# Top-32 selection of two heads in turns, and another order of the work behind the last heads

## The reference, cut

```python
scores = einsum('bthd,bghd->bhtg', Q, K) / sqrt(DH)       # 4 heads of 32, 2048 context rows
topv, topi = top_k(scores, 32); probs = softmax(topv)
attn_mean = zeros_like(scores).at[..., topi].set(probs).mean(axis=1)
c_t = einsum('btg,bgd->btd', attn_mean, x_vision @ Wv)
x = layernorm(x_text)
scale_in, shift_in = split(c_t @ W_film_in + b_film_in)
x = x * (1 + mod_gate * scale_in) + mod_gate * shift_in
K = 2 * einsum('dn,dnl->dl', dC, exp(dtA * arange(L))).real
y = irfft(rfft(x) * rfft(K)) + x * D_skip
scale_out, shift_out = split(c_t @ W_film_out + b_film_out)
y = y * (1 + mod_gate * scale_out) + mod_gate * shift_out
```

## Time and profile before

| what | value |
|---|---|
| median of three runs | 783.0 us (781.75 to 784.87) |
| the profiled execution | 782.62 us, span 780.8 us |
| busy share PE, DVE, ACT, POOL | 87%, 48%, 35%, 29% |
| chain that ended last | PE 63%, DVE 16%, POOL 9%, ACT 6%, issue 3%, DMA 2% |
| mean granted TensorE clock | 0.906 |

### The profile page before, as it was taken

How to read it: one execution, slowest core, us unless ns; L and a number is a source line. 1 busy time by engine, 2 the same in 40 slices (tenths; PEclk the granted TensorE clock), 3 DMA queues, 4 the chain that set the end, 5 groups by cost and what they waited for, 6 DMA issues and landing times.

```text
span 780.8 us, 10116 instructions
## 1 busy us (share of the span) xinstructions
PE 681.5 (87%) x3848; PEld 320.2 (41%) x3848; DVE 374.8 (48%) x1179; ACT 273.1 (35%) x580; POOL 227.5 (29%) x146
## 2 busy tenths in 40 slices
PE   4948659878478799999999999989799999999997
PEld 2314235334244354444444444545554333333343
DVE  5988879998997335561002341534662111001114
ACT  1867868879778110013120001545111001111010
POOL 2479767856957920000000000000140000000012
PEclk9976677868568899999999999999799999999999
DMA  9971320702704851006005014001958999999923
GB/s 289 292 280 40 107 82 7 263 1 83 281 0 161 264 222 40 1 0 216 0 7 209 0 39 177 1 1 47 384 199 303 389 375 346 372 373 369 382 80 126
DMA packets 63521, 132.94 MB, mean 170 GB/s; under 512 B 8368, under 2 KB 18544, under 8 KB 62960
## 3 DMA queue, kind: packets, MB, share of 16 engines
q1 hardware_dynamic: 59072, 122.91, 43.6%
q0 software_dynamic: 1920, 6.29, 2.8%
q10 hardware_dynamic: 2480, 3.08, 1.2%
HBM read 121.86 MB, written 8.32 MB: 167 GB/s over the span
## 4 chain that ended last, share of the span: by engine, by line
PE 63%; DVE 16%; POOL 9%; ACT 6%; issue 3%; DMA 2%; ACTq 0%; DVEq 0%; POOLq 0%
PE PS L1675 8%; PE PS L1650 7%; PE PS L1471 7%; PE PS L1491 7%; PE PS L1389 6%; PE PS L1243 4%; DVE KA L949 4%; PE PS L1508 4%; PE PS L1670 4%; PE PS L1655 4%; DVE AR L990 2%; PE PS L1505 2%; POOL TT L434 2%; PE PS L1319 1%; DVE V L958 1%
## 5 line engine op out<-in xcount | busy, mean ns | idle before, releaser
L415 POOL TENSOR_TENSOR RS<-VE,CST 128x1 f32<-128x1 f32 (+1 forms) x18 | 11.2, 621 | 268.7 <-DVE VE L912 266.4
L1276 PE MATMUL PS<-AR,WK 128*128 128x512 f32 x96 | 54.7, 726 | 17.3 <-DMA AR<-in_ctxT 17.3
L949 DVE MAX8 KA<-AR 128x8 f32<-128x64 f32 x512 | 66.4, 210 | 2.4 <-issue 2.0
L1214 DVE COPY AR<-PS 128x512 f32<-128x512 f32 (+1 forms) x9 | 5.9, 668 | 124.3 <-PE PS L1243 124.3
L1675 PE MATMUL PS<-AR,TT 128*32 128x512 f32 x512 | 60.3, 593 | 1.5 <-issue 1.4
L567 POOL DMA_INDIRECT AR<-expert_rows,SLU x8 | 8.3, 1034 | 181.0 <-DMA expert_rows<-XT 178.9
L1650 PE MATMUL PS<-AR 128*32 128x512 f32 x512 | 57.9, 594 | 0.9 <-ACT AR L863 0.6
L1471 PE MATMUL PS<-TT,AR 128*128 128x512 f32 (+2 forms) x144 | 55.5, 546 | 3.3 <-ACT TT L791 3.3
L1293 PE MATMUL PS<-AR,QT 32*128 32x512 f32 x128 | 43.3, 759 | 16.8 <-ACT AR L600 15.9
L1389 PE MATMUL PS<-AR 128*128 128x512 f32 x128 | 56.1, 594 | 0.3 <-DVE XT L1115 0.3
L1491 PE MATMUL PS<-AR 128*128 128x512 f32 x128 | 55.5, 593 | 0.9 <-ACT AR L800 0.9
(11 more groups left out here) (290 smaller groups left out, 1205.7 us busy)
## 6 DMA issues: line engine op xcount, KB each, us to landing
AR<-in_w SPq DMA_DIRECT2D x32, 2048.0 KB, 12.4
AR<-in_ctxT SPq DMA_DIRECT2D x16, 768.0 KB, 8.1
AR<-in_ctx SPq DMA_DIRECT2D x16, 768.0 KB, 7.9
AR<-in_W SPq DMA_DIRECT2D x2, 4096.0 KB, 12.9
token_rows<-AR SPq DMA_DIRECT2D x1, 2560.0 KB, 11.0
X<-in_x SPq DMA_DIRECT2D x2, 1024.0 KB, 5.5
AR<-AR POOLq DMA_DIRECT2D x8, 256.0 KB, 3.4
AR<-in_W_film_in SPq DMA_DIRECT2D x4, 512.0 KB, 11.4
```

The source lines that it names most:

```text
L949: last = eng.max(CAND[0][:, n, :], s[:, n * G // NCH:(n + 1) * G // NCH])
L1276: last = mm(PS[:, 4 + n % 2, :], WK[:, j, :], CXT[slot][:, j, :], start=j == 0, stop=j == KV - 1)
```

## The change

It does five things.

1. The two heads of a pair are selected together. `thresholds(m, found)` alternates between them, with candidates in CAND[0] and CAND[1] and what is left in LEFT[0] and LEFT[1] (in KB); `Chain.put` signals, `Chain.after` waits later. VectorE's order in a pass is maxima of the first head, `whole` in late passes, a masked product of the pair before, maxima of the second head, the other masked product, `diagonal` in late passes, thresholds, settle.
2. `exponentials` makes both heads' scaled maxima and both logarithms with one instruction each; the two shifts follow each other without a wait.
3. At the end VectorE does masked(14) and masked(15) ahead of last_powers, and modulate(0) ahead of diagonal(3). ScalarE does the text norm of batch 0 ahead of exponentials(7), attended(2) ahead of lag_sizes(3), and step_sizes(3) only behind the copies of CTT. GpSimd's step values of the last quarter come behind gains(0) and the last two heads' sums. On TensorE film_in(0) and attended_rows(3) come ahead of lags(3).
4. The input bias has its own columns (BFI, two places) and is loaded once the last turns are there; its gates come ahead of the other three text norms. The output bias is loaded behind the last step values and just ahead of K's store, and its gates come behind the copy of CC.
5. The context rows of batch 3 wait for the last swap instead of the last step values.

```diff
-        CAND = [KA[:, n * 256:(n + 1) * 256].rearrange("p (a b) -> p a b", b=8) for n in range(2)]
+        CAND, LEFT = ([v[:, n * 256:(n + 1) * 256].rearrange("p (a b) -> p a b", b=8) for n in range(2)]
+                      for v in (KA, KB))
-        BFI, BFO = at(29696, 2, D), at(30720, 2, D)
+        BFI, BFO = [at(12800, D), at(34304, D)], at(30720, 2, D)
...
@@ SP
-            eng.wait_ge(S_["steps"], 4)
-            for v, a in ((BFI, "b_film_in"), (BFO, "b_film_out")):
-                load(v.rearrange("p a b -> p (a b)"), I[a].partition_broadcast(P), "ld_bf")
+            eng.wait_ge(S_["turn"], 4)
+            for n in range(2):
+                load(BFI[n], I["b_film_in"][n * D:(n + 1) * D].partition_broadcast(P), "ld_bf")
+            eng.wait_ge(S_["swap"], 32 * 4)
             eng.wait_ge(S_["cc_ps"], 3)
             load_ctx(3)
...
+            eng.wait_ge(S_["steps"], 4)
+            eng.wait_ge(S_["ld_bf"], 32)
+            load(BFO.rearrange("p a b -> p (a b)"), I["b_film_out"].partition_broadcast(P), "ld_bf")
             kv = kdram.rearrange("(g d) (a m) -> (d a) g m", d=16, m=LB)
             eng.wait_ge(S_["diag"], 4)
...
@@ GpSimd
+            def step_values(q):
+
                 eng.wait_ge(S_["trig"], 2 * q + 2)
...
                     magnitudes(q)
+                    if q < 3:
+                        step_values(q)
+            step_values(3)
             for b in range(1, B):
                 gains(b)
...
@@ ScalarE
-                for i, v, a in pair:
-                    link(eng.activation(a[:, 0:1], v[:, 0:1], ACT.Copy, scale=-SCALE))
+                two = slice(2 * m % 4, 2 * m % 4 + 2)
+                link(eng.activation(SM[:, two, 0], V32[:, two, 0], ACT.Copy, scale=-SCALE))
                 for i, v, a in pair:
                     link(eng.activation(EV[:, :], v, ACT.Exp, bias=a[:, 0:1], scale=SCALE, accum_out=a[:, 1:2]))
+                link(eng.activation(SM[:, two, 2], SM[:, two, 1], ACT.Ln, scale=float(XH)))
                 for i, v, a in pair:
-                    link(eng.activation(a[:, 2:3], a[:, 1:2], ACT.Ln, scale=float(XH)))
-                for i, v, a in pair:
-                    link(eng.activation(a[:, 3:4], a[:, 2:3], ACT.Identity, bias=a[:, 0:1], scale=-1.0))
+                    last = link.put(eng.activation(a[:, 3:4], a[:, 2:3], ACT.Identity, bias=a[:, 0:1], scale=-1.0))
+                link.after(last)
...
+                if m == NPH:
+                    eng.wait_ge(S_["nb"], 1)
+                    eng.wait_ge(S_["masked"], NT - 3)
+                    text_norm(0)
                 if 2 <= m:
                     exponentials(m - 1)
...
-                    lag_sizes(q)
-                    if q:
-                        step_sizes(q)
                     if q == 3:
                         attended(2)
+                    lag_sizes(q)
+                    if 1 <= q < 3:
+                        step_sizes(q)
...
+            step_sizes(3)
+            eng.wait_ge(S_["ld_bf"], 32)
+            eng.activation(BFI[0], BFI[0], ACT.Identity, bias=c("one"), scale=MG[:, 0:1]).then_inc(S_["gate"], 1)
+            eng.activation(BFI[1], BFI[1], ACT.Copy, scale=MG[:, 0:1]).then_inc(S_["gate"], 1)
...
+            eng.wait_ge(S_["ld_bf"], 48)
+            eng.activation(BFO[:, 0, :], BFO[:, 0, :], ACT.Identity, bias=c("one"), scale=MG[:, 0:1])\
+               .then_inc(S_["gate"], 1)
+            eng.activation(BFO[:, 1, :], BFO[:, 1, :], ACT.Copy, scale=MG[:, 0:1]).then_inc(S_["gate"], 1)
             eng.wait_ge(S_["kt2_ps"], 1)
...
@@ VectorE
+            def thresholds(m, found):
...
+                ready = found
                 for r in range(TOPK // 8):
+                    best = []
+                    for (v, c0, left, _), n in zip(heads, ready):
+                        link.after(n)
+                        best.append(link.put(eng.max(v[:, 8 * r:8 * r + 8], left if r else c0)))
                     if r == TOPK // 8 - 1:
                         break
+                    ready = []
+                    for (v, c0, left, _), n in zip(heads, best):
+                        link.after(n)
+                        ready.append(link.put(eng.match_replace(out=left, in_to_replace=v[:, 8 * r:8 * r + 8],
+                                                                in_values=left if r else c0, imm_value=TAKEN)))
...
+            for m in range(NPH):
+                q, late = divmod(m, 2)
+                found = [chunk_maxima(2 * m)]
+                if q and late:
+                    whole(q)
+                if m:
+                    masked(2 * m - 2)
+                found.append(chunk_maxima(2 * m + 1))
+                if m == 0:
                     whole(0)
+                if m:
+                    masked(2 * m - 1)
+                if q and late:
                     diagonal(q - 1)
+                thresholds(m, found)
+                settle(m)
+            masked(NT - 2)
+            masked(NT - 1)
+            last_powers()
...
+            eng.wait_ge(S_["gate"], 2)
+            modulate(0)
             diagonal(3)
             eng.wait_ge(S_["gate"], 4)
-            modulate(0)
             eng.wait_ge(S_["ld_k"], 16)
...
@@ TensorE
+            film_in(0)
+            attended_rows(3, range(4))
             lags(3)
-            film_in(0)
             transform(0)
-            attended_rows(3, range(4))
             context_rows(3)
```

More of the change, by code:

```diff
@@ new lines, in thresholds @@
+                done = []
+                for (v, c0, left, counts), n in zip(heads, best):
+                    link.after(n)
+                    done.append(link.put(eng.tensor_scalar(left, c0, v[:, TOPK - 1:TOPK], 0.0, ALU.is_ge, ALU.add,
+                                                           accum_out=counts[:, 0:1])))
+                for j, (v, c0, left, counts) in enumerate(heads):
+                    link.after(done[j])
+                    last = link.put(eng.tensor_scalar(left[:, 0:NCH], CAND[j][:, :, 7], v[:, TOPK - 1:TOPK], 0.0,
+                                                      ALU.is_ge, ALU.add, accum_out=counts[:, 1:2]))
```

60 lines of the change are left out of this document (16 added, 44 removed).

## The result

The changed kernel takes 785.69 us (783.81 to 787.64, 18 runs), the kernel before 782.76 beside it: ratio 1.0036, 95% interval 1.0026 to 1.0046. It is 0.36% slower, clear of 1 by its interval but inside the 0.5% called no change above, and 4 us over the upper end of my range. The profiled execution took 787.32 us, span 785.5, where the earlier trace rows belong to a span of 780.8.

The account below looks back on a forecast made before the run. VectorE and ScalarE were taken to bound the first 281 us in alternation. Last exponentials 231.2 plus an unchanged stretch of 41.5 put the spectra at 272.7, 8.4 earlier: 783.0 - 8.4 = 774.6 us, 80% range 767.5 to 781.5.

Parts of the forecast that it names:

- K's trip through DRAM: Before the spectra: K's store (8 us), load (3.1) and add (1.1) end with the context rows, cancelling the reordering's gain.
- Turns: VectorE's selection: alternating the two heads' thresholds hides waits between instructions, 2.0 us a pair, 16 over eight pairs.
- Rival A: Selections in turns give nothing; only the shorter exponentials act, 780.1 us; chance 0.14.
- Exponentials: ScalarE, start of small exponentials to first wide one: 1.9 us instead of 2.47, with fewer copies, logs and waits.
- How much of it arrives: Walk through the head passes: half of the 16 us is lost in waits for ScalarE; last exponentials 8.35 us earlier.
- a fixed 18.1: Even pass: GpSimd's powers, lags, turns and last key copies follow the masked product in an unchanged 18.1 us.
- E(7): Start of ScalarE's small exponentials for pair 7, the last; forecast at 231.2 us, 8.35 earlier than 239.55.
- Sums done at +19.6: GpSimd's last two sums, 7.1 + 5.7 us, end 19.6 us behind the last small exponentials' start; before, 25.5.
- Powers on VectorE end at +15, hidden: The last powers, behind the masked products, end 15 us after the last small exponentials' start and cost nothing.
- Step values, lags, transform: After the sums: step values at +24.3, lags until +26.2, transform 1.4 us, context rows ending at +38.2 to +40.2.
- rival C: K's store and reload decide the end: 782.3 us at its old length; chance 0.19, of it 0.07 for slower.
- hidden while K is last, 1.3 if the context rows are: Output bias gates ahead of ScalarE's copy of K's columns: no cost if K comes last, otherwise 1.3 us.

Follow-up runs that it names:

- before_again: The kernel before, unchanged, submitted once more as a kernel of its own; ratio 1.0015.
- a_gate: Changed kernel with VectorE's wait for all four bias gates moved from ahead of K's first-lag add to behind it; ratio 1.0025.
- a_gate2: a_gate with ScalarE's two output bias gates also put behind its copies of K's columns and of the context columns; ratio 0.9996.
- b_turns_exps: Kernel before with only the selections in turns, their order of masked products and the shorter exponentials, its end untouched; ratio 0.9930.
- a_nopow: a_gate2 without the last quarter's powers, only a subtraction of 8 columns left, so that quarter of K is missing; ratio 0.9945.
- a_steps: a_powers with the last quarter's step sizes ahead of attended(2) and its step values ahead of the sums, as in the kernel before; ratio 0.9974.
- b_norm: b_turns_exps with the text norm of batch 0 ahead of the last exponentials; ratio 0.9924.
- b_norm_mod: b_norm with modulate(0) ahead of diagonal(3), bias gates ahead of the other norms, the wait for all four behind K's addition; ratio 0.9919.
- a_pe: a_steps with TensorE's order undone: lags(3), film_in(0), transform(0), then attended_rows(3) and context rows; ratio 0.9935.
- a_powers: a_gate2 with the last powers ahead of the two last masked products and lag_sizes(3) ahead of attended(2); ratio 0.9932.
- b_turns_exps2: b_turns_exps repeated unchanged in the last group; ratio 0.9939.

## Why the prediction was wrong, point by point

Three steps failed: that GpSimd's work in an even pass keeps its length when VectorE's masked product moves beside it, that the last powers are hidden behind the masked products, and that the gates cost at most 1.3 us. K's trip through DRAM, which the prediction had decide, decided nothing. In the order of the prediction:

**Turns: right.** 1.44 us a round, starts 0.33 to 0.38 apart where 0.33 to 0.41 was named, and the 2.0 us a pair are there. The Trainium skill's rule of "The DRAIN you can't avoid" (in "VectorE: DVE Perf Modes"), that leaving out semaphores gains nothing, does not hold for these operations: 0.33 us from maximum to maximum without a wait, ratio 0.9964 for the turns alone. The section itself adds that a next operation that is not held back starts earlier, which the prediction left out and the trace bears out. Rival A had 0.14 and fell.

**Exponentials: right.** 1.87 us from E(5) to the first wide exponential (187.70 to 189.57), 1.9 forecast, 2.47 before.

**"How much of it arrives": wrong, 8.35 forecast.** The walk treated GpSimd's powers, lags and turns behind the even pass's masked product as "a fixed 18.1". The change moves the second masked product from behind a threshold to right behind the second head's maxima, beside the last of those products (4.38 us for 2.35, in passes 4 and 6). The part list had it that "the order of masked products and chunk maxima stays" and counted only the threshold that moved: the instructions were the same, their neighbours on the other engine were not. With that product moved, E(7) saved 6.2 to 7.2 us against before_again; with it as it is, 3.8 to 4.0 in a_gate and a_gate2. At E(3) 2.2 had come in b_turns_exps (133.67 for 135.84) where 3.8 were forecast; no run explains that part. Nor can I assign the remaining 2.5 between a_gate and the 1.25 of the first profiled execution; in pass 1 alone E(1) varied between 76.6 and 78.4 with the same code up to there.

**First masked product and sums: terms mis-sized.** "+3.9" was +3.9. "Sums done at +19.6" was +22.15: the sums took 7.70 and 6.42 where 7.1 and 5.7 stood, and started at +7.9 where these terms leave +6.8, behind gains of which the second took 3.20 us for 1.27. "Powers on VectorE end at +15, hidden" was the failing step: they ended at +20, and their cover was itself the sums. Ahead of the masked products they would have filled VectorE's idle time. I had named it as gain that the masked product "waited until 249.37" for them; in b_turns_exps, where the powers start at E+1.3 and not at E+3.8 as before, this wait is 2.4 us.

**Step values, lags, transform: order right, sizes short.** The sum had lags and transform between the last transposes and the context rows, and there they were. Lags ran at +27.8 to +29.7, where they were to start at +24.3 and end at +26.2: 2.55 of the delay is that of the sums, 0.9 the step values (2.81 and 2.79 us for 2.35 each). The transform held TensorE for 2.8 us where 1.4 stood, at a granted clock of 0.64 behind the lags' 0.50. So the context rows ended at +42.9, forecast +38.2 to +40.2.

**K's trip: wrong, and the decisive sentence with it.** 8 us taken for the store, bounds 7 and 12.3; it took 4.5, outside the bounds. 106 GB/s had been read from a stretch that other transfers shared: 0.54 MB moved there from 262.5 to 268.0 us, the store is half of it, and alone it ran at 87 GB/s for 3 us. The sum also slipped: +27.8, 8, 3.1 and 1.1 make +40.0, not +40.3. "The reordering is paid back in full by K's trip through DRAM" is false, and rival C, which rested on it, is too, although a time like the one measured stood in it: K was on the chip at E+38.6, the context rows ended at +42.9, and K waited 6.3 us for the gates. That the kernel came out slower, as C had it at 0.07, is luck and no support for it.

**The gates: missed.** "hidden while K is last, 1.3 if the context rows are" looked at ScalarE only. VectorE's wait for the fourth gate stands in program order ahead of K's addition, and moving the gate behind the CC copy moved that addition behind the context rows. With the clock it cost 3 us, ratio 0.0040. The rule for an added wait, who is queued behind it, was not applied to a wait that stays in place while its signal moves.

**The sum.** 8.4 us at the spectra were forecast; they came 4.0 late. The 12.4 between are 7.1 at E(7) and 5.3 behind it (46.8 for 41.5), of this 2.7 by the gates and 2.65 on the way to the context rows, against a stretch forecast as unchanged (the context rows give 0.1 back); the spectra's lower clock adds 0.95 behind them. The 0.73 for faster put too much on a walk that took the engines one by one.

## What to carry to other kernels

When an instruction moves, look up what the other engine runs at its new place: two-input products of VectorE and GpSimd go one after the other, and the one that loses stretches by the other's length. Check each wait whose signal moves as if it were new, with everything queued behind it. Fill an engine's wait with work before moving it (the last powers, lags and transform were free where they were), and change the order of all engines together or of none.

## What the hardware showed that I had not expected

- A masked product of 2048 columns on VectorE takes 2.35 us alone and 6.67 behind two products of GpSimd that follow each other at once; GpSimd's product of 1024 columns takes 2.35 alone and 4.38 behind VectorE's. The one that is second does not get in between two that follow at once.
- Even a subtraction of 8 columns waits: in a_nopow it lasts 2.33 us and ends with GpSimd's sum beside it (248.30, where the next sum starts at 248.22).

```profile
245.97 2.33 DVE L1089 TENSOR_TENSOR AR<-AR 128x8 f32<-128x8 f32 x1
```

- Where both engines' products fill the same stretch, their order hardly matters: a_steps, b_norm, b_norm_mod and a_pe end their sums at E+23.1 to E+23.2, as b_turns_exps does, whether the gains stand ahead of or behind the powers. Only less work ahead of the sums ends them sooner: a_powers, without the step values there (4.7 us), at E+19.8.
- Storing K, 256 KB in 4112 small packets, took 4.5 us with nothing in front (87 GB/s while it moved), in the changed kernel and the eleven made from it, and 12.3 behind 5 MB of other loads.
- The same context rows took 10.48 to 10.59 us in most profiled executions (granted clock 1.00 in b_turns_exps and b_norm_mod), 12.59 to 13.03 in three at 0.81 to 0.84 (b_norm, a_pe, b_turns_exps2), two of them behind a wait of TensorE for the sums of 2.5 us; b_norm_mod had the same wait and 10.59. One profiled execution doesn't settle 2 us here; the intervals do.
